# A two-layer graph kernel on one Trainium2 core: features loaded once, in the order of the transposed blocks, and the adjacency rows of the first sweep in that order too

## What is computed

```python
def layer0(X, H):                          # H is adj, 4096 x 4096
    msg = H.T @ X
    return msg * (1 / H.sum(axis=0))[:, None]     # inf becomes 0

def layer1(x, adj, W, b):
    x1 = swish((adj @ x) @ W + b)
    return swish((adj @ x1) @ W + b)

h = relu(layernorm(x));  x = x + layer0(h, adj)       # x is 4096 x 128
h = relu(layernorm(x));  x = x + layer1(h, adj, W, b)
```

## Time and profile before

| | |
|---|---|
| runs | 651.44, 652.76, 654.67 us |
| profiled execution | 653.19 us |
| its span, first to last instruction | 651.3 us |
| mean granted TensorE clock | 0.992 |
| PE busy | 627.0 us (96%) |
| POOL busy | 562.0 us (86%) |
| DVE busy | 504.0 us (77%) |
| ACT busy | 298.5 us (46%) |
| DMA | 199.82 MB, mean 307 GB/s |

### The profile page before, as it was taken

How to read it: one execution, slowest core, us unless ns; L and a number is a source line. 1 busy time by engine, 2 the same in 40 slices (tenths; PEclk the granted TensorE clock), 3 DMA queues, 4 the chain that set the end, 5 groups by cost and what they waited for, 6 DMA issues and landing times.

```text
span 651.3 us, 6791 instructions
## 1 busy us (share of the span) xinstructions
PE 627.0 (96%) x2232; PEld 402.9 (62%) x2232; DVE 504.0 (77%) x518; ACT 298.5 (46%) x372; POOL 562.0 (86%) x283
## 2 busy tenths in 40 slices
PE   7889999999997989999999999999999999999996
PEld 5356666567574456566667667666666666665664
DVE  3988889888847889687777877777787968966982
ACT  1475433543442164645445445445444435433452
POOL 2389899499786579998999999999999999996994
PEclk8999999999998999999999999999999999999999
DMA  8999999999999999999999999909999999999971
GB/s 269 355 374 333 338 336 361 312 328 358 325 280 342 288 343 348 331 315 286 347 347 311 348 347 323 281 2 217 313 346 333 324 318 343 343 320 292 327 234 33
DMA packets 155827, 199.82 MB, mean 307 GB/s; under 512 B 5520, under 2 KB 138896, under 8 KB 155792
## 3 DMA queue, kind: packets, MB, share of 16 engines
q1 hardware_dynamic: 91568, 136.07, 66.4%
q10 hardware_dynamic: 64224, 63.32, 33.0%
HBM read 197.26 MB, written 2.10 MB: 306 GB/s over the span
## 4 chain that ended last, share of the span: by engine, by line
PE 65%; POOL 16%; issue 8%; DMA 6%; DVE 3%; ACT 1%; SPq 1%; POOLq 0%; DVEq 0%; ACTq 0%
PE dg L391 23%; POOL a_lo L762 12%; PE dg L408 11%; PE dg L398 10%; PE dg L397 10%; PE m_ps L314 5%; DMA raw<-in_adj_dram 4%; POOL at_lo L776 3%; PE m_ps L417 2%; DMA h<-in_x_dram 2%; PE m_ps L319 1%; PE m_ps L334 1%; DVE dg L614 1%; PE m_ps L320 1%; POOL norm L743 1%
## 5 line engine op out<-in xcount | busy, mean ns | idle before, releaser
L776 POOL TENSOR_TENSOR at_lo<-turned,at_hi 128x1024 fp32r<-128x1024 f32 x160 | 379.9, 2413 | 18.7 <-ACT at_hi L509 12.3
L658 DVE STREAM_TRANSPOSE turned<-raw 128x1024 f32<-128x1024 f32 x256 | 302.4, 1222 | 79.1 <-PE dg L391 43.4
L509 ACT ACTIVATE at_hi<-turned 128x1024 fp32r<-128x1024 f32 x160 | 169.1, 1060 | 201.3 <-DVE turned L658 147.2
L391 PE MATMUL dg<-turned,f_w 128*128 128x512 f32 x384 | 180.5, 592 | 3.0 <-issue 1.8
L762 POOL TENSOR_TENSOR a_lo<-raw,a_hi 128x1024 fp32r<-128x1024 f32 x62 | 145.8, 2383 | 34.7 <-ACT a_hi L478 34.4
L614 DVE TENSOR_TENSOR dg<-raw,dg 128x2048 f32<-128x2048 f32 x60 | 137.6, 2293 | 39.4 <-DMA raw<-in_adj_dram 37.6
L397 PE MATMUL dg<-at_hi,f_hi 128*128 128x512 f32 x320 | 133.0, 416 | 0.5 <-ACT at_hi L509 0.5
L408 PE MATMUL dg<-at_lo,f_hi 128*128 128x512 f32 x320 | 130.1, 488 | 1.1 <-POOL at_lo L776 1.0
L398 PE MATMUL dg<-at_hi,f_lo 128*128 128x512 f32 x320 | 126.5, 395 | 0.0
L314 PE MATMUL m_ps<-raw,h 128*128 128x512 f32 x264 | 119.8, 601 | 6.3 <-DMA raw<-in_adj_dram 6.3
L391 PEld LDWEIGHTS dg<-turned,f_w 128*128 128x128 f32 x384 | 72.4, 189 | 58.2 <-issue 50.3
(11 more groups left out here) (50 smaller groups left out, 248.9 us busy)
## 6 DMA issues: line engine op xcount, KB each, us to landing
raw<-in_adj_dram SPq DMA_DIRECT2D x64, 1024.0 KB, 7.8
raw<-in_adj_dram SPq DMA_DIRECT2D x120, 512.0 KB, 11.8
raw<-in_adj_dram ACTq DMA_DIRECT2D x120, 512.0 KB, 12.5
x<-in_x_dram SPq DMA_DIRECT2D x16, 128.0 KB, 8.2
out_dram<-zs SPq DMA_DIRECT2D x12, 128.0 KB, 12.4
h<-in_x_dram SPq DMA_DIRECT2D x1, 768.0 KB, 9.7
h<-in_x_dram SPq DMA_DIRECT2D x1, 256.0 KB, 3.3
out_dram<-zs SPq DMA_DIRECT2D x4, 64.0 KB, 1.8
```

The lines of the kernel that those rows point to most:

```text
L391: mm = pe.matmul(acc, f_w[:, UC * WHOLE3.index(j) + c], turned[:, unit % TURN, c], start=first and c == 0, stop=False)
L509: act.activation(at_hi[:, s % RING3], turned[:, unit % TURN], ACT.Copy).then_inc(hi3_done, 1)
L658: dve.transpose(dst, src).then_inc(t3_done, 1)
L776: pool.tensor_tensor(at_lo[:, s % RING3], turned[:, unit % TURN], at_hi[:, s % RING3].bitcast(f32), ALU.subtract).then_inc(lo3_done, 1)
```

## The change

The features are loaded once, in the head, into `x`, in the order `(q b m c)`: 16 times 4 tiles or 8 tiles to 32 partitions. DVE's statistics and ACT's `relu` read `x` and write `h`; the second loads and their semaphores are gone. For `h` to match, the adjacency rows of sweep 1 must come in the same order: tile (q, m) is made of the rows 1024 q + 256 b + 32 m + c on partition 32 b + c. So `load1` reads from `adj_rows`, whose tile has as source four blocks b, each of 32 rows c, each of 1024 numbers; before, it was 128 rows p, two tiles, 1024 numbers. The destination is 128 partitions in both. A pair is now two transfers of 512 KB, each of which adds 16 to the pair's semaphore, so the waits are for 32 per use.

In the head, pairs 1 and 2 are both issued ahead of the last half of the features (before: one, then features, then the next).

```diff
-    x_tiles = x_in.rearrange("(t p) d -> p t d", p=P)
-    adj_tiles = adj.rearrange("(t p) c -> p t c", p=P)
+    adj_rows = adj.rearrange("(q b m c) n -> q m b c n", b=P // SB, m=QT, c=SB)
...
-                sp.dma_start(raw1[:, v % RAW1], adj_tiles[:, 2 * k:2 * k + 2, q * QC:(q + 1) * QC])\
-                  .then_inc(raw1_loaded[v % RAW1], 16)
-
-            for b, (lo, hi) in enumerate(HEAD):
-                sp.dma_start(h[:, lo:hi], x_tiles[:, lo:hi]).then_inc(x_loaded[b], 16)
-                load1(b)
-            for v in range(len(HEAD), QUARTERS * PAIRS):
+                for i in range(2):
+                    sp.dma_start(raw1[:, v % RAW1, i], adj_rows[2 * k // QT, 2 * k % QT + i][:, :, q * QC:(q + 1) * QC])\
+                      .then_inc(raw1_loaded[v % RAW1], 16)
+
+            def load_nodes(n, q, m0, m1):
+                for b in range(P // SB):
+                    sp.dma_start(x[b * SB:(b + 1) * SB, q * QT + m0:q * QT + m1], x_nodes[q, b][:, m0:m1])\
+                      .then_inc(x_loaded[n], 16)
+
+            load_nodes(0, 0, 0, QT // 2)
+            load1(0)
+            load_nodes(1, 0, QT // 2, QT)
+            load_nodes(1, 1, 0, QT)
+            load1(1)
+            load1(2)
+            load_nodes(2, 2, 0, QT)
+            load_nodes(2, 3, 0, QT)
+            for v in range(3, QUARTERS * PAIRS):
                 load1(v)
                 if v in PIECE0_SP:
                     load3(sp, 0, SP_BLOCKS[PIECE0_SP.index(v):][:1])
-                if v % PAIRS in NODES_AT:
-                    q, b = v // PAIRS, NODES_AT.index(v % PAIRS)
-                    sp.dma_start(x[b * SB:(b + 1) * SB, q * QT:(q + 1) * QT], x_nodes[q, b])\
-                      .then_inc(nodes_loaded[q], 16)
...
-                    pe.wait_ge(raw1_loaded[v % RAW1], 16 * (v // RAW1 + 1))
+                    pe.wait_ge(raw1_loaded[v % RAW1], 32 * (v // RAW1 + 1))
...
-                        relu(h_hi[:, 2 * SPLIT_ROWS.index(k) + t % 2], h[:, t], t)
-                    relu(h[:, t], h[:, t], t).then_inc(h_ready, 1)
+                        relu(h_hi[:, 2 * SPLIT_ROWS.index(k) + t % 2], x[:, t], t)
+                    relu(h[:, t], x[:, t], t).then_inc(h_ready, 1)
...
             def head(b):
-                dve.wait_ge(x_loaded[b], 16)
-                statistics(h, range(*HEAD[b]), b).then_inc(mv_ready, 1)
+                dve.wait_ge(x_loaded[b], 64 if b == 0 else 128)
+                statistics(x, range(*HEAD[b]), b).then_inc(mv_ready, 1)
...
-                if part == 0:
-                    dve.wait_ge(nodes_loaded[q], 16 * (P // SB))
```

More of the change, by code:

```diff
@@ L23 @@
 SPLIT_ROWS = (6, 8, 9, 11, 12, 14) + LATE_ROWS
-NODES_AT = (3, 6, 9, 12)
 SB = 32
@@ L120, in build @@
         x_loaded = [sem(f"x_loaded{b}") for b in range(len(HEAD))]
-        nodes_loaded = [sem(f"nodes_loaded{q}") for q in range(QUARTERS)]
         w_loaded, b_loaded = sem("w_loaded"), sem("b_loaded")
@@ L471, in hi1 @@
             def hi1(v):
-                act.wait_ge(raw1_loaded[v % RAW1], 16 * (v // RAW1 + 1))
+                act.wait_ge(raw1_loaded[v % RAW1], 32 * (v // RAW1 + 1))
                 for i in range(2):
@@ L601, in head @@
             def head(b):
-                dve.wait_ge(x_loaded[b], 16)
-                statistics(h, range(*HEAD[b]), b).then_inc(mv_ready, 1)
+                dve.wait_ge(x_loaded[b], 64 if b == 0 else 128)
+                statistics(x, range(*HEAD[b]), b).then_inc(mv_ready, 1)
             def add_degrees(v):
                 src = raw1[:, v % RAW1]
-                dve.wait_ge(raw1_loaded[v % RAW1], 16 * (v // RAW1 + 1))
+                dve.wait_ge(raw1_loaded[v % RAW1], 32 * (v // RAW1 + 1))
                 if v % PAIRS == 0:
```

## The result

The changed kernel takes 1132.32 us (median of 4 runs, 1126.64 to 1134.9), the kernel before 652.92 us beside it: 1.729 times as long (95% interval 1.721 to 1.738). The profiled execution took 1126.64 us, with a span of 1124.7 us and a mean granted clock of 0.823.

A forecast was written before the change was run, and what follows sets the result against it. Sweep 1 was taken as bound by PE, with some 15% to spare in transfers; on four engines, start, pairs, features, blocks and last matmuls end at 681.8 us, sweeps 2 and 3 bring the span to 1100.5, forecast 1102, range 1040 to 1500.

The forecast's parts named there:

- four engines at their old speed: Sweep 1's pairs: 4 engines at 25.6 GB/s each, 102 GB/s, 10.2 us a pair; with rates down to 16, chance 0.80.
- Both rivals with 16 engines: Sweep 1: work dealt by rows, 647 us, chance 0.05; or 16 engines with features choking the head, 661 us, chance 0.05.
- the one that the four hinder each other: Sweep 1's pairs: four engines at 12.5 GB/s each, 21 us a pair, 1801 us total; chance 0.08.
- the one that they are faster alone: Sweep 1's pairs: one engine alone does twice 25.6 GB/s, 5.1 us a pair, about 775 us total; chance 0.02.
- 64 pairs: Sweep 1's pair transfers on four engines: 64 x 10.23 us = 654.8 us.
- features of the head: Other features, 1.84 MB, 224 packets for each engine at 25 ns: 5.7 us; at 88 ns 19.7.
- blocks of sweep 2 beside the last pairs: Piece 0 and ACT's blocks of pieces 1 and 2: 8 transfers of 512 KB, 1.28 us each, 10.2 us.
- last pair's matmuls: End of sweep 1: 8 matmuls at half clock, 0.86 us each, 6.9 us.
- sweeps 2 and 3: As in the kernel before, 417.0 us, plus 1.7 us for 3.3 us at half clock at most.
- PE's clock: Granted clock near 0.5 through sweep 1, as PE idles more than 3 us before every pair.
- Issue to landing: Sweep 1: a 512 KB transfer takes 40 us or more from issue to landing, since five pairs are queued.
- The gain of the first rival: Sweep 1 with work dealt by rows to 16 engines: 652.8 - 6 = 647 us; chance 0.05.

The follow-up runs named there:

- two, four and eight blocks: Kernel before, pairs as two 512 KB transfers whose source has two, four or eight blocks of rows outermost: 1758.48, 1145.86 and 823.43 us.
- The run with the late pieces: Changed kernel, but SP and ACT wait for the last pair's landing before issuing pieces 1 and 2 of sweep 2: 1097.36 us.
- the run with the rows of before: Changed kernel, but each pair is loaded as before, 128 rows outermost in one 1 MB transfer: 653.52 us.
- The run with moved loads: Kernel before, with the 16 loads of `x` behind pairs 16 to 46 instead of pairs 3, 6, 9 and 12 of each quarter: 648.08 us.
- Sixteen blocks of 8 partitions: Kernel before, pairs as two 512 KB transfers whose source has 16 blocks of 8 rows outermost: 734.46 us.

## Why the prediction was right, and where its sum was off

The forecast was 1102 us, the range 1040 to 1500, the likeliest case's own 1075 to 1250, and slower had 0.93. Measured: 1132. The case was the one called likeliest, four engines at their old speed, and its main signs are in the trace: 105 GB/s and a share of 0.26 (102 and 0.26 were named), additions 10 us apart, each behind a wait for a transfer. Other signs missed. PE's waits in sweep 1 sum to 339 us (174.3 for transfers, 164.8 put down to ACT), where some 400 were named; its clock, the time from issue to landing and the time of sweeps 2 and 3 are below. Both rivals with 16 engines (647 and 661 us) fall with the share; the one that the four hinder each other (12.5 GB/s each) and the one that they are faster alone fall with the 26 GB/s, which two, four and eight blocks repeat.

The terms, from the additions in DVE's timeline. The features and the blocks are what is left when the pairs are taken off. Pair 3 is added at 57.54, pair 48 at 507.77, pair 61 at 650.48, pair 63 at 685.60. Between 3 and 48 a pair takes 450.23 / 45 = 10.005 us.

| term | forecast | measured | from |
|---|---|---|---|
| start | 4.2 | 4.2 | taken as forecast |
| 64 pairs | 654.8 | 640.3 | 64 x 10.005 |
| features of the head | 5.7 | 13.3 | 57.54 - 4.2 - 4 x 10.005 |
| blocks of sweep 2 beside the last pairs | 10.2 | 27.8 | 142.71 - 13 x 10.005, and 35.12 - 2 x 10.005 |
| last pair's matmuls | 6.9 | 5.0 | 690.60 - 685.60 |
| sweeps 2 and 3 | 418.7 | 434.1 | 1124.7 - 690.60 |
| span | 1100.5 | 1124.7 | |

- **The pairs** are 14.5 us under the sum. I had taken 25.6 GB/s from windows with all 16 engines at work; the four do 26.2.
- **The features** cost 7.6 us more. DVE's waits, at the start and for pieces two and three:

```profile
4.92 0.88 DVE L600 BATCH_NORM_STATS2 stats<-x 128x6 f32<-128x128 f32 x4 [4.92 <-DMA x<-in_x_dram]
...
21.58 2.42 DVE L600 BATCH_NORM_STATS2 stats<-x 128x6 f32<-128x128 f32 x12 [15.37 <-DMA x<-in_x_dram]
...
47.46 3.19 DVE L600 BATCH_NORM_STATS2 stats<-x 128x6 f32<-128x128 f32 x16 [20.34 <-DMA x<-in_x_dram]
...
57.54 2.30 DVE L619 TENSOR_TENSOR dg<-raw,dg 128x2048 f32<-128x2048 f32 x1 [1.09 <-DMA raw<-in_adj_dram]
```

  The step that failed is "I take 5.7, since 12 engines run ahead and the four have the partitions to themselves". The packets of the features were nearly as quick as I took them: from 4.2 to 57.5 us those of 512 B take 31 ns (mean), 7.0 us for an engine's 224. But the pairs' own packets became slower beside them, 180 ns instead of 159.5: for the 256 that four pairs give an engine that is 5.3 us more. Together 12.3 of the 13.3 us. The 88 ns that I had named as the other end hide the same thing: where a load of `x` passes, its packets take 37 ns and those of 4 KB 269.
- **The blocks beside the last pairs** cost 17.6 us more, the largest miss. I priced them at 1.28 us each, with 21 us for all eight at the 200 GB/s rate as the other end. They took 3.5 us each, more than either. Here too the pairs' packets grew: their mean is 169 ns from 507.8 to 650.5 us and 229 from there to 685.6, instead of 159.5, which is 15.7 us for each of the four engines. The blocks' own 256 packets of 1 KB for an engine come to 11.8 us at 46 ns, their median up to 650.5 us; this is an estimate, as the trace doesn't say which engine had a packet. The run with the late pieces, where neither queue has blocks of pieces 1 and 2 beside the last pairs, ends sweep 1 16.3 us sooner.
- **Sweeps 2 and 3** were "as now, 417.0 us, plus 1.7". They take 434.1. The same run brings 12.6 of the 17.1 us back by a wait, and no such loss follows where the last pairs run on 16 engines. So what was in flight at the change of stage is the cause of most of it, and not PE's clock, which is at 1.00 in the windows above. I had written that if sweeps 2 and 3 are slow too, the cause is another; that was wrong: a shape in sweep 1 can leave a debt in sweep 2. With most of both debts removed the kernel is at 1097 us, 5 from the forecast, but that is partly luck, as the pairs' -14.5 us and the features' +7.6 stand in it. So is part of the 30 us between 1102 and 1132: without the pairs' -14.5 it would be 45.
- **PE's clock** was to be near 0.5 through sweep 1 and was 0.74 and 0.72. It cost next to nothing here, since PE waits anyhow; only behind the last pair does it count, where its 8 matmuls take 5.1 us, not 3.6, and there DVE's sums end at about the same time (690.4). With two blocks, where PE works 16 of 60 us, it was 0.57.
- **Issue to landing** was to be 40 us or more "since five pairs are queued". From 200 to 600 us the median is 21.9 us. SP's issues themselves take longer instead: in the changed kernel, least, median and most in ns,

```profile
L268 SPq DMA_DIRECT2D raw<-in_adj_dram x128: 531/4794/11783, 2.6 to 646.0; - x128
```

  where an issue took 0.44 to 0.49 us at the start of the kernel before and those of its pairs have a median of 0.37. So my "64 more issues of 0.44 us" was wrong tenfold, and harmless: SP waits in its own issue for the four engines, and has nothing else to do.
- **The gain of the first rival** (6 us, without the loads of `x`) did not come in the run with the rows of before: 653.5 us. In its trace PE stands 1.0 us behind the kernel before in mid-sweep (144.41 to 143.40) and 1.9 ahead at the end of sweep 1 (232.36 to 234.29). So the head, where I had 1.6 us of gain, loses 1.0, as the later features take 2.3 us; the last quarter, where I had 4.5, gains 2.9. The run with moved loads gains 2.9 and 2.5 us in the same two parts. In both traces the last quarter is quicker without the loads of `x`, though the longest stall stays. These are single traces, and the medians of the run with the rows of before show no gain; that of the moved loads (5 us, 0.9%) is clear in the medians too.

## What to carry to other kernels

When a transfer's source is rearranged, read the shape of both sides as the instruction carries them: if their outermost dimensions are 4 and 128, a quarter of the engines works, though the bytes and the size of the packets are the same. While transfers are queued without a gap, the DMA share of a window divided by the share with all engines at work tells the part of the engines that works. Splitting the transfer into parts of 32 rows and 32 partitions brought all 16 engines back, but not their rate (739 us, where 128 rows to 128 partitions have 653). Where transfers of different kinds follow each other, count what is in flight when the stage changes: a wait that holds the next stage's loads back made the changed kernel 35 us faster. And price a transfer that runs beside others by what it does to their packets too: here that was 5.3 of 12.3 us in the head and more than half of the 27.8 at the end of sweep 1.

## What the runs showed of the hardware that I had not expected

- Sixteen blocks of 8 partitions keep all 16 engines busy (1.04) and still bring 242 GB/s instead of 410. Eight blocks of 16 partitions lose nothing (206 GB/s at 0.53). By the rule of the Trainium skill that p and p + 32 share a port (page "SBUF — State Buffer", section "Door 1: The DMA port swizzle"), engines that go through their blocks in step would meet in pairs on a port with sixteen blocks, which could explain 242; but with eight they would meet too, with no loss. What decides it stays open.
- An engine does 25 to 27 GB/s with 4 KB packets (159 to 164 ns for each) whether 2, 4, 8 or, with 128 rows outermost, 16 of them work; the idle ones give nothing to the others.
- A packet of 4 KB becomes slower beside transfers to 32 partitions: 269 ns (mean) beside a load of `x`, 309 beside the first block of piece 0, 229 beside the blocks at the end of the changed kernel's sweep 1, though only four engines carry the pairs there.
- In sweep 2 of the changed kernel, with a mean busy share of 1.11 and every slice at nine tenths or more, the rate goes from 208 to 351 GB/s. The share says that engines have packets, not that they are fast.
